# A vision-transformer layer on one core: new orders for four engines, the up/gate contraction cut into 128 + 64 rows, and W loaded by one queue

## The reference

```python
p = img2patches(x)                                  # [32, 36, 768]
h = layernorm(p, ln1_g, ln1_b) @ W + b              # 768 -> 192
h = layernorm(h, ln2_g, ln2_b)
# attention over the 32 images at each patch position: 12 heads of 16
q, k, v = split(_layernorm(h) @ in_proj_weight.T + in_proj_bias)
attn = softmax(normalize(q) @ normalize(k).T * exp(min(logit_scale, LOGIT_MAX)))
h = h + ((attn @ v) * head_scale) @ out_w.T + out_b
# feed-forward with quantized activations (8 bit) and weights (-1, 0, 1)
up, gate = split(bitlinear(_layernorm(h), w_in, g_in))     # 192 -> 2 x 512
h = h + bitlinear(silu(gate) * up, w_out, g_out)           # 512 -> 192
```

## Time and profile before

| what | value |
|---|---|
| median of 3 runs | 126.59 us |
| the three runs | 126.52, 126.59, 135.68 us |
| span of the profiled execution, first to last instruction | 124.5 us |
| granted TensorE clock, mean | 0.988 |
| busy: TensorE, VectorE, ScalarE, GpSimd | 110.0, 104.1, 80.5, 73.4 us |

### The profile page before, as it was taken

How to read it: one execution, slowest core, us unless ns; L and a number is a source line. 1 busy time by engine, 2 the same in 40 slices (tenths; PEclk the granted TensorE clock), 3 DMA queues, 4 the chain that set the end, 5 groups by cost and what they waited for, 6 DMA issues and landing times.

```text
span 124.5 us, 4809 instructions
## 1 busy us (share of the span) xinstructions
PE 110.0 (88%) x1904; PEld 90.6 (73%) x1904; DVE 104.1 (84%) x338; ACT 80.5 (65%) x179; POOL 73.4 (59%) x172
## 2 busy tenths in 40 slices
...
GB/s 95 244 191 152 190 182 162 123 178 208 297 79 0 5 0 0 5 5 5 0 8 0 5 0 5 0 5 5 0 5 34 5 0 21 44 8 49 51 50 48
DMA packets 24509, 7.68 MB, mean 62 GB/s; under 512 B 20579, under 2 KB 23909, under 8 KB 24486
## 3 DMA queue, kind: packets, MB, share of 16 engines
...
## 4 chain that ended last, share of the span: by engine, by line
PE 51%; DVE 17%; POOL 11%; ACT 8%; issue 6%; DMA 4%; DVEq 0%; POOLq 0%
PE bank L747 10%; PE bank L769 7%; PE bank L770 6%; PE bank L793 4%; DMA w_emb_sb<-in_L_tok_W_dram 4%; PE bank L781 3%; PE bank L829 3%; PE bank L655 3%; PE bank L727 2%; PE bank L669 2%; POOL yw L447 2%; PE bank L662 2%; ACT sq L576 2%; DVE ss L985 1%; PE bank L810 1%
## 5 line engine op out<-in xcount | busy, mean ns | idle before, releaser
L747 PE MATMUL bank<-w_emb_c,xT 128*128 128x192 f32 x108 | 19.3, 328 | 0.0
L747 PEld LDWEIGHTS bank<-w_emb_c,xT 128*128 128x128 f32 x108 | 17.4, 190 | 0.1
L655 PE MATMUL bank<-ones 128*128 128x128 f32 x84 | 13.1, 316 | 1.2 <-POOL ones L327 1.0
L379 POOL TENSOR_TENSOR rs<-mv,mhalf 128x1 f32<-128x1 f32 x9 | 5.1, 575 | 14.4 <-DVE mv L953 14.4
L655 PEld LDWEIGHTS bank<-ones 128*128 128x128 f32 x84 | 12.2, 227 | 1.8 <-POOL ones L327 1.0
L769 PE MATMUL bank<-w_qkv,xhT 97*128 97x384 f32 (+1 forms) x36 | 12.1, 417 | 1.6 <-DVE qkp L1022 1.5
L770 PE MATMUL bank<-w_qkv,xhT 96*128 96x384 f32 (+1 forms) x36 | 11.7, 405 | 0.0
L829 PE MATMUL bank<-wi_t,xqT 96*128 96x512 bf16 x36 | 9.3, 380 | 2.1 <-ACT xqT L600 1.9
L447 POOL TENSOR_TENSOR yw<-yy,gout_bc 128x512 f32<-128x512 f32 x8 | 10.2, 1273 | 0.6 <-DVE yy L1095 0.3
L769 PEld LDWEIGHTS bank<-w_qkv,xhT 97*128 97x128 f32 x36 | 6.1, 189 | 5.4 <-issue 1.9
L389 POOL TENSOR_TENSOR hg<-h0s,g_bc 128x192 f32<-128x192 f32 x9 | 5.2, 575 | 7.8 <-DVE h0s L960 7.7
...
## 6 DMA issues: line engine op xcount, KB each, us to landing
xs<-in_x_dram SPq DMA_DIRECT2D x32, 96.0 KB, 3.1
...
xs<-in_x_dram ACTq DMA_DIRECT2D x4, 96.0 KB, 5.8
...
w_emb_sb<-in_L_tok_W_dram SPq DMA_DIRECT2D x1, 288.0 KB, 3.4
w_emb_sb<-in_L_tok_W_dram ACTq DMA_DIRECT2D x1, 288.0 KB, 4.9
```

The lines of the kernel that those rows point to most:

```text
L655: nc.tensor.matmul(spare_bank, ones[:, :], ones[:, :], start=True, stop=True)
L747: mm = nc.tensor.matmul(emb_bank, xT[:, t % 3, P * k:P * (k + 1)], w_emb_c[:, 3 * (k % 2) + k // 2, :], start=(k == 0), stop=(k == KF - 1))
```

## The change

Nine things change, all in the lists and in a few steps:

1. Loads: SyncE issues both halves of W, then the image. ScalarE issues b1, g1 and b first, then its four image transfers; before it issued half 1 of W, g1, the image transfers, then b1 and b.
2. TensorE's list starts with 12 unused matmuls (`fill(0)` to `fill(5)`) instead of 25, and `bmm_` stands ahead of `cmm_`. Over the whole list the unused matmuls fall from 53 to 24; `warm_` is gone.
3. VectorE runs `wv_` before `c_row_set`, and `bst0_` before `wc_`.
4. ScalarE copies tile 0 channel by channel in the order 1, 0, 2, and `tab_` goes to the end of its list.
5. `ff1` contracts 192 rows as 128 + 64: two matmuls over 128 rows, then one over rows 64 to 127 (gate) and one over rows 0 to 63 (up). `wi_t` and `xqT` are laid out for that; rows 64 to 127 of the second transpose hold the last 64 features.
6. `wiT_` has 16 transposes as before, in another layout; `wiE_` is two activations of 1024 and 512 columns instead of 2 x 1024.
7. `ms2_` may carry an extra wait, as `ysq_` does.
8. All four engines have new orders for the steps of the middle and the end.
9. GpSimd's list has the same steps in a new order: `rs1_(1)` and `rs3_(0)` earlier, `c_idb_set`, `lsd_` and `whs_` later.

```diff
+            load_emb(sp, 1)
...
-            load_emb(act, 1)
+            load_column(act, b1_sb, ln1_b, ld_b1)
             load_column(act, g1_sb, ln1_g, ld_g1)
+            act.dma_start(b_emb_row[:, :], b_emb.rearrange("(a n) -> a n", a=1)).then_inc(ld_b1, 16)
             load_half_rows(act, 0, 0, (3,), ld_x0)
             load_half_rows(act, 0, 1, (2, 3), ld_x1)
             load_half_rows(act, 0, 2, (3,), ld_x2)
-            load_column(act, b1_sb, ln1_b, ld_b1)
...
+                nc.scalar.activation(wi_t[:, 0:2 * FF], bank[2].bitcast(I16)[:, :], ACT.Identity, bias=mround[:, 0:1]).then_inc(p_wiE, 1)
+                nc.scalar.activation(wi_t[:, 2 * FF:3 * FF], bank[3].bitcast(I16)[:, 0:FF], ACT.Identity, bias=mround[:, 0:1]).then_inc(p_wiE, 1)
...
+                nc.tensor.transpose(xqT_bank[:, 0, :], low_half(xq[:, t % 3, 0:P]), ident_b[:, :])
+                nc.tensor.transpose(xqT_bank[:, 1, :], low_half(xq[:, t % 3, DR:D]), ident_b[:, :]).then_inc(xqT_ps, 1)
...
-                for half, dst in ((1, gate_ps), (0, up_ps)):
-                    for c in range(2):
-                        mm = nc.tensor.matmul(dst[:, :], xqT[:, t % 3, c, :], wi_t[:, c, FF * half:FF * (half + 1)], start=(c == 0), stop=(c == 1))
-                mm.then_inc(ff_ps, 1)
+                nc.tensor.matmul(gate_ps[:, :], xqT[:, t % 3, 0, :], wi_t[:, FF:2 * FF], start=True, stop=False)
+                nc.tensor.matmul(up_ps[:, :], xqT[:, t % 3, 1, :], wi_t[:, 0:FF], start=True, stop=False)
+                nc.tensor.matmul(gate_ps[:, :], xqT[DR:P, t % 3, 1, :], wi_t[DR:P, 2 * FF:3 * FF], start=False, stop=True)
+                nc.tensor.matmul(up_ps[:, :], xqT[0:DR, t % 3, 0, :], wi_t[0:DR, 2 * FF:3 * FF], start=False, stop=True).then_inc(ff_ps, 1)
...
-            fill(0); fill(1); fill(2); fill(3); fill(4); fill(5); fill(6); warm_(); cmm_(); bmm_(); xTl(0); fill(7)
+            fill(0); fill(1); fill(2); fill(3); fill(4); fill(5); bmm_(); cmm_(); xTl(0); fill(6); xTh(0)
...
-            wrow_(); wneg_(); c_row_set(); wv_(); wc_(); xpd(1); bst0_(); xpd(2); bst1_(0); mv1_(0); bst1_(1)
+            wrow_(); wneg_(); wv_(); c_row_set(); bst0_(); wc_(); xpd(1); bst1_(0); bst1_(1); mv1_(0); mv1_(1); mv0_()
```

More of the change, by code:

```diff
@@ L467, in _ @@
             c_ones_set(); c_div_set(); z_id_set(); c_id_set(); c_pad_set(); c_round_set(); c_eps_set(); c_vx_set()
[L468 to L471, removed]
@@ L640, in _ @@
+            xqTe(7); ysq_(6); yqTe(3); th_(7); yqTe(4); xq_(8); yq_(5); xqTe(8); ysq_(7); yqTe(5); th_(8); yq_(6); yq_(7)
+            yqTe(6); ysq_(8); yqTe(7); yq_(8); yqTe(8); tab_()
             store(act, T - 1, (2, 3))
@@ L643, in _ @@
         def _(pe):
-            def warm_():
-                pe.wait_ge(c_ones, 1)
-                for k in range(11):
-                    nc.tensor.matmul(spare_bank, ones[:, :], ones[:, :], start=True, stop=True)
             def fill(t, *freed):
@@ L870, in _ @@
+            ff1(7); yqT_(4, (yqT_ok, 4)); ff2(3, (out_ok, 3)); xqT_(8, (yy_ok, 4)); ff2(4, (out_ok, 4)); yqT_(5); ff1(8)
+            ff2(5, (out_ok, 5)); yqT_(6); fill(10, (out_ok, 6)); ff2(6, (out_ok, 6)); yqT_(7); ff2(7, (out_ok, 7)); yqT_(8)
+            fill(11, (out_ok, 8)); ff2(8, (out_ok, 8))
         @block.vector
@@ L1148, in _ @@
-            on_(6); qkn_(7); h2_(5); yg_(3); bst4_(5); ax4_(4); mv4_(5); qT_(7); ri4_(4); xc_(5); qs4_(4); kT_(7)
-            ax4_(5); h2_(6); ri4_(5); ss_(8); qs4_(5); bst4_(6); ax5_(2); out_(0); mv4_(6); mx_(7); ssm_(8); ri5_(2)
-            xc_(6); ng_(8); qs5_(2); sm_(7); ax5_(3); np0_(8); ax4_(6); np1_(8); yg_(4); np2_(8); ri4_(6); yy_(4)
-            np3_(8); pT_(7); qkn_(8); qs4_(6); kT_(8); qT_(8); yg_(5); rsum_(7); yy_(5); on_(7); mx_(8); ri5_(3)
-            sm_(8); ax5_(4); qs5_(3); pT_(8); h2_(7); out_(1); bst4_(7); ri5_(4); mv4_(7); qs5_(4); xc_(7); rsum_(8)
@@ L1153, in _ @@
-            ax4_(7); on_(8); ri4_(7); yg_(6); qs4_(7); yy_(6); out_(2); ax5_(5); h2_(8); bst4_(8); ri5_(5); mv4_(8)
-            xc_(8); ax4_(8); qs5_(5); ri4_(8); yg_(7); qs4_(8); yy_(7); out_(3); ax5_(6); ri5_(6); out_(4); qs5_(6)
-            ax5_(7); ri5_(7); qs5_(7); out_(5); yg_(8); yy_(8); out_(6); ywd(8); ax5_(8); ri5_(8); qs5_(8); out_(7)
-            out_(8)
+            wrow_(); wneg_(); wv_(); c_row_set(); bst0_(); wc_(); xpd(1); bst1_(0); bst1_(1); mv1_(0); mv1_(1); mv0_()
+            xpd(2); biasc_(); h0s_(0); lsm_(); bst1_(2); mv1_(2); h_(0); bst3_(0); mv3_(0); h0s_(1); xhd(0); h_(1)
```

158 lines of the change are left out of this document (79 added, 79 removed).

## The result

The changed kernel took 126.95 us at the median of 20 runs (124.77 to 131.81), the kernel before 126.74 beside it (125.85 to 135.68). The ratio is 0.992 (95%: 0.989 to 0.995): 1.0 us faster, where -2.7 was forecast. That is within 2%, no change by the bound used here. The ratio leaves the longer runs of either kernel out, ten of the changed kernel's 20 and its profiled run of 129.3 us (span 127.5) among them; with all runs in, the two medians are the same. The late rows of this trace, from 95 us on, show what can happen in the kernel and not what the ratio is made of.

A forecast was written before the change was run, and what follows sets the result against it. VectorE was taken as the bound, with a slow start. Start -2.0, middle -0.4 and end -0.3 sum to -2.7: span 121.8 from 124.5, plus 2.1 to the median run, 123.9 us; range 121.9 to 127.6.

The forecast's parts named there:

- The start: Before 35 us: `h0s_(0)` at 16.2 against 18.27, VectorE's work about 2.0 us ahead; term -2.0, bounds -0.8 and -2.8.
- if it streams twice as fast: Load of W on SyncE: landing at 4.9 at double rate, 5.6 at the mean rate; 5.2 was taken.
- The third image group: Image loads: lands at 30.0 to 30.4 whatever the start gained, so `bst1_(6)` can move up by 1.4 to 1.8.
- `wv_` directly behind `wrow_`: Sign of being right, VectorE's start: `wv_` ahead of the memsets, ending at 8.8 instead of 10.8.
- The middle: 35 to 110 us: shorter `ff1` and new orders together give -0.4, out of at most 2.7 us of VectorE's idle time.
- +1.5 as the bound for new holes: Middle: a new order may open holes, up to +1.5, half of what VectorE idles there now.
- I count both at nothing: Removing twelve unused matmuls at 94.15 to 96.99 (0.1 at most) and six at 108.6 changes nothing.
- The rival of the lower clock: Without late unused matmuls TensorE falls to 1.2 GHz and bounds the end: 4.5 us more, 128.4 us; chance 0.12.
- four passes in about 0.8: Sign of being right, `ff1`: its four passes, 1.02 long before, take about 0.8 with 128 + 64.
- at worst nothing: `ff1`'s 64-row pair side by side saves 0.21 per tile, 1.9 us of TensorE's time over nine tiles; at worst nothing.
- -0.2 by the Trainium skill's rule: Middle: tiling-mode changes drain TensorE twice per tile, so `ff1`'s share could vanish, leaving -0.2 instead of -0.4.
- The end: `yg_(8)` ahead of `out_(5)` and a shorter `ff1(8)`, against two more ScalarE activations: -0.3, from -0.6 to +0.4.

The follow-up runs named there:

- the 124.0 us run: Traced run of the changed kernel with GpSimd's `yyp(1)` and `yw_(2)` each one place later; median 126.11 us, ratio 0.978 to the kernel before.
- both rows short: Changed kernel with GpSimd's `s4_(2)` ahead of `yyp(0)` and `an5_(1)` ahead of `yw_(2)`; 125.43 us, ratio 0.985 to the kernel before.

## Why the prediction was wrong

The direction was right, the size wrong: -1.0 for -2.7.

**The start: right in mechanism, under-sized.** `h0s_(0)` at 15.37, not 16.2; -2.9 instead of -2.0, at the bound. W on one queue landed at 4.71, better than the 4.9 of "if it streams twice as fast", and the bias product started at 5.50, so b came with W. The third image group didn't cap it: `bst1_(6)` started at 30.34 with no wait ahead of it, in the 30.0 to 30.4 forecast for the landing, and the steps around it in the list were 2.75 us ahead. "`wv_` directly behind `wrow_`" held; `ss_(1)` came at 31.64 for 32.4.

**The middle: the failed step.** -0.4 was the term; of the 2.9 us of the start 1.7 were left at the last `out_` in the 124.0 us run, and 0.6 if the `rn` of 86 us, short in that run, is put back with its 1.1 us: an estimate, and near the 1.0 measured. "With at most 2.7 us of holes in the middle I take -0.4", with +1.5 as the bound for new holes. The argument counted VectorE's busy time as fixed work, since it has the same steps. It isn't fixed: 2.2 us of it in the kernel after (0.81 before) is `rn` standing beside GpSimd's products of 512 columns, booked as busy, and 0.35 more is the `rn` of 27 us. One such row was in the profile of before, at 77.51, and I read `rn` nowhere. That is +1.4 of the missing 1.7 plus the start's extra 0.9, 2.6 us in all. The runs bear it out in kind (both rows short, ratio 0.992 to 0.985; 0.995 in the kernel before), in size only in part: 0.9 us for 2.1 us of shorter rows between 0.992 and 0.985, with intervals that overlap. Two more losses don't hang on the clock: the hole at 49 us, in every trace of the new lists (0.41 to 1.01 us of TensorE's time) and in none of the old, and the 0.75 us of the weight's transposes, in every trace with the 128 + 64 form. These and the `rn` rows overlap with waits of other kinds and needn't add up; no run splits them. That the middle had "at most 2.7 us of holes" to give was right; that a new order would leave them as they are had no ground.

**The unused matmuls: counted at nothing, wrongly argued.** "Their removal brings 0.1 at most ... I count both at nothing." The wait for `yy_(4)` behind them was read rightly, and I took from it that they cost nothing and so are worth nothing. The second doesn't follow: without them the kernel before is 3.0 us slower by the ratio (1.024). The rival of the lower clock named them, looked only at the six of 108.60, and had 0.12. In the kernel after the loss is avoided in part of the runs: the new list puts `pv(7)`, `sc(8)` and `ff2(0)` in their place, and the 124.0 us run, without one of the calls, has the clock at 1.00 until 117. So for the ratio of -1.0 the term of nothing came out about right, by luck, since the reason given for it was wrong. With the calls where TensorE waits, the ratio didn't move (0.991) as long as `rn` was blocked, and went from 0.985 to 0.982 once it was free, which is inside the intervals. With the old `ff1` the clock's fall is plain to see and its absence too (127.8 and 125.3 at the median).

**`ff1`.** "Right: four passes in about 0.8": the pair does run side by side, 0.39 us for both at 64.08, but it starts 0.31 behind the pass ahead of it and not 0.21. With both `rn` rows short the four passes run from 63.55 to 64.47, 0.92 us, so half of the 1.9 us of TensorE's time that I counted doesn't appear. "That they fill 128 rows instead of 96 costs nothing in rows I can see" was wrong for the weight's transposes, 0.75 us on the path to `ff1(0)`, and so was the bound "at worst nothing". -0.2 by the Trainium skill's rule was nearer than -0.4, and the measured value is nothing (0.992 and 0.993), or a loss in the traces.

**The end.** -0.3 didn't show. VectorE's last wait is 2.17 for 2.30, and 2.29 in the 124.0 us run, where VectorE idles 3.4 us behind 110 instead of 2.9.

What stays open: how much of the 2.6 us each of these losses takes in a typical run of the kernel after, and why such a block comes some 8 us late in some runs. No edit was tried that removes the holes. Nor do the runs split the late loss of the kernel after into clock and order.
